# More filling products on TensorE between the end of the expert search and the first expert's rows

## The chip, the cores and the metric

The kernel runs on one core of one Trainium2 chip. The metric is the device time in microseconds (us) of one execution. One execution was also recorded by the hardware profiler; its rows are what this text reads. Five engines work side by side: PE (TensorE, matrix products; PEld is its weight load), DVE (VectorE), ACT (ScalarE), POOL (GpSimd, which here also issues the gathers) and SP (SyncE, which issues plain DMAs).

## The reference

A small language-model layer: embedding, attention, then a mixture of experts in which each expert chooses its tokens. What matters here is the last part (cut):

```python
N = B * S                                    # 8 * 512 = 4096 tokens, D = 256
k = max(MIN_CAPACITY, ceil(N * 2.0 / E))     # E = 8 experts, k = 1024
scores = softmax(xt @ Wr)
G, idx = top_k(scores.T, k)                  # each expert takes its 1024 best tokens
X_in = xt[idx]
h = gelu(einsum('ekd,edh->ekh', X_in, W1) + b1)       # 256 -> 1024
X_e = einsum('ekh,ehd->ekd', h, W2) + b2              # 1024 -> 256
out = zeros.at[idx].add(G * X_e)
```

## The kernel before, in words

`build_attention` does the attention and takes the first 60% of the time. `build_middle` does the router, the choice of tokens and the experts. Each engine has a hand-written list of instructions; they meet only through semaphores, and each engine works through its own list strictly in the order written. The part that the change touches runs from about 775 to 800 us of the span, in these steps:

1. **Search.** DVE and ACT count scores above a threshold; PE adds the counts over partitions (`total`, L1524) in 14 rounds. After each round PE does three filling products.
2. **Ranks.** PE multiplies once more (L1591, semaphore `ranked`), DVE computes ranks (`marked`), PE transposes them (L1597, semaphore `turned`).
3. **Lists.** For expert 0, DVE and ACT write two one-hot tensors (`hot_a`, `hot_b`), and PE turns them into a list of token numbers with 32 small products into `l_ps` (`write_list`, L1605, semaphore `listed`). DVE copies the list out (L1309 to L1316, semaphore `tok_ready`), and only then may it and PE do the same for expert 1.
4. **Rows.** As soon as a list is there, POOL issues eight indirect DMAs of 128 rows each (`gather`, L1036). The first four of expert 0 have a semaphore each (`first_in0` to `first_in3`), on which PE waits.
5. **First turn.** `first_turn` transposes each 128 rows on PE (L1625) into `x_ps` and `up`. ACT copies them out as the high part of a split float (L1415, `e_xT0hi`), DVE forms the low part (L1322, `e_xT0lo`).
6. **Experts.** For each of 16 steps of an expert PE does `up` (six products of 512 columns; `first_up`, L1636, for the first step, L1650 after it) and, two steps later, `down` (twelve products of 256 columns, L1662). Between them ACT applies Gelu twice (L1495 `hid`, L1498 `hT_hi`) and DVE forms `hT_lo` (L1322). Step 2's `up` waits for step 0's `hT_hi`, step 3's for step 1's.

The filling products are `warm(n)`: n products of the first expert's weights with themselves, 128x128 by 128x512, into the bank `y_ps[0][1]`. Nobody reads the result and nobody waits for it; the bank is written anew when the experts start. They show as `L1520 y<-w_0hi` in the trace. They wait for nothing, but PE's list is in order, so whatever stands behind them waits until they are through.

Of the kernel before, what the change touches and what calls it, by code (L numbers as in the profile page):

```python
# [802 lines left out]
def build_middle(nc, a, ident, h2, x2, wr_pair, early_lT, score, score_rows, shared):  # L803

    ctx = ExitStack()
    with ctx:
# [101 lines left out]
        def after(eng, name, count):  # L908

            if isinstance(count, int) and count <= 0:  # L910
                return
            eng.wait_ge(s[name], count)
# [593 lines left out]
        def _(pe):  # L1506
# [10 lines left out]
            def warm(n):  # L1517

                for _ in range(n):
                    nc.tensor.matmul(y_ps[0][1][:], w1[0][0][:, 0, 0:P], w1[0][0][:, 0, 0:HALF],  # L1520
                                     start=True, stop=True)

            def total(which, n):
                return nc.tensor.matmul(l_ps[:, 0:n], groups[:, which, :], count_bf[:, 0:n],  # L1524
                                        start=True, stop=True)
# [54 lines left out]
            for r in range(ITERATIONS):  # L1580
                pe.wait_ge(s["act_counted"], r + 1)
                for n in range(2):
                    nc.tensor.matmul(l_ps[:, 2:3], groups[:, 2, :], count_act[:, n:n + 1],
                                     start=n == 0, stop=n == 1)
                pe.wait_ge(s["counted"], r + 1)
                total(0, 2).then_inc(s["totalled"], 1)
                warm(3)
            pe.wait_ge(s["counted"], ITERATIONS + 1)
            for k, terms in enumerate([((0, 0), (1, 1)), ((1, 0), (1, 1))]):
                for n, (which, col) in enumerate(terms):  # L1590
                    last = nc.tensor.matmul(l_ps[:, 4 + k:5 + k], groups[:, which, :],  # L1591
                                            count_bf[:, col:col + 1], start=n == 0, stop=n == 1)
            last.then_inc(s["ranked"], 1)
            warm(12)
            pe.wait_ge(s["marked"], 1)
            for c in range(2):
                last = nc.tensor.transpose(x_ps[:, c * P:(c + 1) * P], rank[:, c, :], ident[:])  # L1597
            last.then_inc(s["turned"], 1)

            def write_list(e):  # L1600

                after(pe, "hot_ready", e + 1)
                after(pe, "tok_ready", e)
                for t in range(NB):
                    last = nc.tensor.matmul(l_ps[0:LIST_A, 0:2 * LIST_A], hot_a[:, t, :],  # L1605
                                            hot_b[:, t, 1:3, :].rearrange("p k b -> p (k b)"),
                                            start=t == 0, stop=t == NB - 1)
                last.then_inc(s["listed"], 1)
# [10 lines left out]
            def first_turn():  # L1619

                for c in range(TB):
                    warm(2)
                    pe.wait_ge(s[f"first_in{c}"], 16)
                    for kt in range(KT):
                        last = nc.tensor.transpose(first_x_ps[kt][:, c * P:(c + 1) * P],  # L1625
                                                   got[0][:, c, kt * P:(kt + 1) * P], ident[:])
                        if c == TB - 1:
                            last.then_inc(s["e_xt_tr"], 1)
                warm(2)
# [36 lines left out]
                            stop=dt == DT - 1 and c % 2 == 1 and n == 2)  # L1666
                last.then_inc(s["down_done"], 1)

            warm(16)
            pe.wait_ge(s["hot_b0"], 1)  # L1670
            write_list(0)
            warm(18)
            write_list(1)
            first_turn()

            def body(e, i, more, more2):
                for t in range(STEPS):
                    if t == 0:
                        after(pe, "w_lo2", 2 * e + 2)
                        if e > 0:  # L1680
                            after(pe, "e_xt_lo", 4 * e + 1)
                    if t == DT:
                        after(pe, "e_xt_lo", 4 * e + 4)
                    if e == 0 and t == 0:
                        first_up()
                    else:
                        up(e, i, t)
                    if e == E - 1 and t >= DT + LAG:
                        continue
                    if t >= LAG:  # L1690
                        down(e, i, t - LAG)
                    elif not (isinstance(e, int) and e == 0):
                        down(e - 1, 1 - i, STEPS + t - LAG)
                    if more2 and t == (4 if e == 0 else 2):
                        write_list(e + 2)
                    if more and 11 <= t < 15:
                        turn(e + 1, 1 - i, t - 11)
                    if e == 0 and t in (5, 6):
                        turn(0, 0, t - 3)
            experts(pe, body)  # L1700
            e = E - 1
            after(pe, "y_b2", e * 4)
            for c in range(TB):
                for dt in range(DT):
                    t = DT + dt
# [69 lines left out]
```

## Time and profile before

| | us |
|---|---|
| three timed runs | 1199.5, 1201.84, 1203.94 |
| median | 1201.84 |
| the profiled execution, its own time | 1200.93 |
| its span, first to last instruction | 1198.7 |

So 2.2 us of the profiled execution lie around its span. A timeline row gives the start in us from the start of the span, how long the row lasts, engine, line, operation, what is written and read, the shape, and the count of merged instructions; in brackets stands the idle time of the engine just before, and what ended it. PE rows overlap, since products are pipelined, and their ends are modelled. PEclk is the granted TensorE clock, 1.00 for 2.4 GHz and 0.50 for 1.2 GHz.

### The profile page before, as it was taken

What the parts mean: (1) busy time and instruction counts of PE and PEld (TensorE: products, weight loads), DVE (VectorE), ACT (ScalarE), POOL (GpSimd) and SP (SyncE); (2) the same over time, 40 slices, a digit from 0 to 9 for tenths busy, and PEclk for the clock granted to TensorE, in tenths of its full rate; (3) what the DMA queues carried; (4) which work ended last, traced back from release to release, by engine and by line L of the source; (5) the groups of instructions that cost most, each with busy time, mean ns of one, the idle gap of its engine ahead of it and who ended that gap; (6) DMA issues with size and microseconds to landing.
All of it is one profiled execution on the core that took longest, in us unless ns stands there. A gap on an engine that the chain in (4) does not pass through costs nothing. (4 is left out here: it accounts for less than half of the span.)

```text
span 1198.7 us, 20289 instructions
## 1 busy us (share of the span) xinstructions
PE 1142.1 (95%) x7083; PEld 999.6 (83%) x7083; DVE 818.8 (68%) x1972; ACT 720.7 (60%) x1533; POOL 825.4 (69%) x926
## 2 busy tenths in 40 slices
PE   3899999999999999999999998878999999999997
PEld 2788888888888888888888885558999999999996
DVE  4787887887887887887887766854555554554433
ACT  3667677677686686676676765315465555555642
POOL 3897898897897897897997864052484574654425
PEclk9999999999999999999999999789999999999999
DMA  5000100100100100100101003321362442523223
GB/s 197 1 18 2 45 28 1 45 27 1 45 27 2 45 28 1 54 18 9 63 1 36 19 1 112 110 66 39 94 138 32 115 124 32 130 39 104 32 23 36
DMA packets 42213, 58.12 MB, mean 48 GB/s; under 512 B 8896, under 2 KB 34944, under 8 KB 41984
## 3 DMA queue, kind: packets, MB, share of 16 engines
q0 software_dynamic: 13824, 21.24, 9.9%
q1 hardware_dynamic: 28288, 35.58, 8.8%
q8 instruction: 57, 0.93, 0.3%
q14 instruction: 44, 0.36, 0.1%
HBM read 35.71 MB, written 16.91 MB: 44 GB/s over the span
## 5 line engine op out<-in xcount | busy, mean ns | idle before, releaser
L278 ACT ACTIVATE prob<-prob,row_min 128x512 f32<-128x512 f32 (+3 forms) x256 | 141.8, 557 | 108.3 <-DVE row_min L468 108.3
L1322 DVE TENSOR_TENSOR hT_lo<-hid,hT_hi 128x512 fp32r<-128x512 f32 x124 | 86.2, 695 | 172.9 <-ACT hT_hi L1498 156.1
L1495 ACT ACTIVATE hid<-up,b_e 128x512 f32<-128x512 f32 x128 | 88.1, 688 | 158.9 <-PE up L1650 138.7
L214 POOL TENSOR_TENSOR q_sin<-q_sin,rope_t 128x512 f32<-128x512 f32 x64 | 82.8, 1293 | 84.0 <-ACT q_sin L302 84.0
L206 POOL TENSOR_SCALAR prob<-prob,row_inv 128x512 f32<-128x512 f32 (+3 forms) x256 | 134.5, 540 | 7.9 <-DVE row_inv L481 5.9
L1036 POOL DMA_INDIRECT x<-routed_rows,tokens x64 | 80.7, 1262 | 79.6 <-DVE tokens L1316 38.1
L403 DVE TENSOR_TENSOR pT_lo<-bank,pT_hi 128x384 fp32r<-128x384 f32 (+1 forms) x192 | 110.7, 596 | 18.4 <-ACT pT_hi L260 17.2
L1047 POOL TENSOR_SCALAR y<-y,gate 128x256 f32<-128x256 f32 x60 | 32.2, 548 | 127.1 <-issue 126.3
L1056 POOL DMA_INDIRECT out<-y,tokens x60 | 98.6, 1643 | 16.2 <-issue 13.9
L682 PE MATMUL bank<-ident,prob 128*128 128x128 f32 x640 | 101.9, 274 | 4.8 <-POOL prob L206 4.7
L260 ACT ACTIVATE pT_hi<-bank 128x384 fp32r<-128x384 f32 (+1 forms) x192 | 96.4, 518 | 13.6 <-PE bank L682 13.3
L468 DVE CUSTOM_DVE_ANT_0 prob<-bank,mask_row 128x512 f32<-128x512 f32 (+2 forms) x192 | 101.4, 554 | 2.0
L621 PE MATMUL bank<-kT_both,qT_hi 128*128 128x512 f32 (+2 forms) x384 | 99.7, 340 | 0.8 <-issue 0.5
L226 POOL TENSOR_TENSOR kT_both<-k_cos,kT_both 128x512 fp32r<-128x512 f32 x64 | 85.1, 1330 | 5.7 <-ACT kT_both L260 5.7
L220 POOL TENSOR_TENSOR q_cos<-q_cos,q_sin 128x512 f32<-128x512 f32 x64 | 82.7, 1293 | 5.0
L621 PEld LDWEIGHTS bank<-kT_both,qT_hi 128*128 128x128 f32 x384 | 71.4, 189 | 17.5 <-DVE row_min L468 1.1
L682 PEld LDWEIGHTS bank<-ident,prob 128*128 128x128 f32 x640 | 75.9, 140 | 11.0 <-POOL prob L206 8.8
L226 POOL TENSOR_TENSOR qT_lo<-q_cos,qT_hi 128x512 fp32r<-128x512 f32 x64 | 83.0, 1298 | 2.9 <-ACT qT_hi L260 2.9
L1498 ACT ACTIVATE hT_hi<-up,b_e 128x512 fp32r<-128x512 f32 x124 | 84.6, 682 | 0.0
L621 PE MATMUL bank<-wo_hi,oT_hi 128*128 128x256 f32 x256 | 81.9, 320 | 2.5 <-DVE oT_lo L403 2.5
L621 PE MATMUL bank<-pT_hi,v_hi 128*128 128x512 f32 (+3 forms) x256 | 82.8, 323 | 0.4 <-DVE pT_lo L403 0.4
L220 POOL TENSOR_TENSOR k_cos<-k_cos,k_sin 128x512 f32<-128x512 f32 x64 | 83.0, 1297 | 0.0
(318 smaller groups left out, 3887.9 us busy)
## 6 DMA issues: line engine op xcount, KB each, us to landing
raw<-in_w SPq DMA_DIRECT2D x16, 1024.0 KB
emb_res<-emb SPq DMA_DIRECT2D x8, 512.0 KB, 3.8
out<-h SPq DMA_DIRECT2D x8, 512.0 KB, 2.9
routed_rows<-x SPq DMA_DIRECT2D x8, 512.0 KB, 3.0
x<-in_wq SPq DMA_DIRECT2D x1, 1024.0 KB
x<-in_wk SPq DMA_DIRECT2D x1, 1024.0 KB, 5.1
x<-in_wv SPq DMA_DIRECT2D x1, 1024.0 KB, 7.3
x<-in_wo SPq DMA_DIRECT2D x1, 1024.0 KB, 10.2
```

The costliest lines, as they stand in the source:

```text
L206: nc.gpsimd.tensor_scalar(pr, pr, row_inv[:, h % 2, k:k + 1], 1.0, ALU.mult, ALU.mult).then_inc(s["norm_done"], 1)
L220: nc.gpsimd.tensor_tensor(cos[:], cos[:], sin[:], ALU.add).then_inc(s[f"{x}_add"], 1)
L226: nc.gpsimd.tensor_tensor(out[1][:, h % 2, :], cos[:], out[0][:, h % 2, :].bitcast(F32), ALU.subtract).then_inc(s[f"{x}_lo"], 1)
L260: nc.scalar.activation(out, in_, ACT.Copy).then_inc(s[name], 1)
L278: nc.scalar.activation(pr, pr, ACT.Exp, bias=row_min[:, h % 2, k:k + 1], scale=-1.0, accum_out=row_sum[:, h % 2, k:k + 1]).then_inc(s["exp ...
L403: nc.vector.tensor_tensor(out, in_, hi.bitcast(F32), ALU.subtract)\
L468: nc.vector.tensor_tensor_reduce(prob[:, h % 2, col:col + w], s_ps[bk][:, pc:pc + w], added, scale=-1.0 / D, scalar=3e38, op0=ALU.add, op1 ...
L621: last = nc.tensor.matmul(out, l, r, start=start and c == 0, stop=stop and c == len(todo) - 1)
L682: last = nc.tensor.transpose(t_ps[f][:, c * P:(c + 1) * P], prob[:, h % 2, col:col + P], ident[:])
L1056: pool.indirect_dma_start(a["out"][:, :], bass.IndirectOffsetOnAxis(tokens[e][:, TB * half + c:TB * half + c + 1], 0), y[half][:, c, :], N ...
L1322: nc.vector.tensor_tensor(out, in_, hi.bitcast(F32), ALU.subtract)\
L1495: nc.scalar.activation(hid[:, t % 2, :], up_ps[t % 2][:], ACT.Gelu, bias=bias)
```

## The change

Seven places get more filling products, 23 in all: 3 between the last search round and the last count, 3 before the transposes of the ranks, 4 before the first list, 5 before the second list, 4 between the products of the second list (one ahead of each eight), and 4 in `first_turn`, one before each of its four waits.

```diff
                 total(0, 2).then_inc(s["totalled"], 1)
                 warm(3)
+            warm(3)
             pe.wait_ge(s["counted"], ITERATIONS + 1)
...
             last.then_inc(s["ranked"], 1)
-            warm(12)
+            warm(15)
             pe.wait_ge(s["marked"], 1)
...
-            def write_list(e):
+            def write_list(e, filled=0):
 
                 after(pe, "hot_ready", e + 1)
                 after(pe, "tok_ready", e)
                 for t in range(NB):
+                    if filled and t % filled == 0:
+                        warm(1)
                     last = nc.tensor.matmul(l_ps[0:LIST_A, 0:2 * LIST_A], hot_a[:, t, :],
...
                 for c in range(TB):
-                    warm(2)
+                    warm(3)
                     pe.wait_ge(s[f"first_in{c}"], 16)
...
-            warm(16)
+            warm(20)
             pe.wait_ge(s["hot_b0"], 1)
             write_list(0)
-            warm(18)
-            write_list(1)
+            warm(23)
+            write_list(1, 8)
             first_turn()
```

The order of the other engines is the same. On PE, this is the stretch from the second list to the first expert's rows before (`y<-w_0hi` are the filling products, `l_ps<-hot_b,hot_a` the list, `x_ps` and `up` `<-ident,x` the transposes):

```order
L1520 MATMUL y<-w_0hi 128x512 x18
L1605 MATMUL l_ps<-hot_b,hot_a 32x64 x32
L1520 MATMUL y<-w_0hi 128x512 x2
L1625 MATMUL x_ps<-ident,x 128x128
L1625 MATMUL up<-ident,x 128x128
L1520 MATMUL y<-w_0hi 128x512 x2
```

And now; one of the 24 at the top stands behind the wait for the second list's one-hots, the other 23 ahead of it:

```order
L1520 MATMUL y<-w_0hi 128x512 x24
L1608 MATMUL l_ps<-hot_b,hot_a 32x64 x8
L1520 MATMUL y<-w_0hi 128x512
L1608 MATMUL l_ps<-hot_b,hot_a 32x64 x8
L1520 MATMUL y<-w_0hi 128x512
L1608 MATMUL l_ps<-hot_b,hot_a 32x64 x8
L1520 MATMUL y<-w_0hi 128x512
L1608 MATMUL l_ps<-hot_b,hot_a 32x64 x8
L1520 MATMUL y<-w_0hi 128x512 x3
L1628 MATMUL x_ps<-ident,x 128x128
L1628 MATMUL up<-ident,x 128x128
```

The list is cut into four, and each pair of transposes has three filling products ahead of it instead of two. From the last search round to the first list, on PE, before (`l_ps<-count_bf,groups` is the last count, `x_ps<-ident,x` the transposes of the ranks):

```order
L1524 MATMUL l_ps<-count_bf,groups 128x2
L1520 MATMUL y<-w_0hi 128x512 x3
L1591 MATMUL l_ps<-count_bf,groups 128x1 x4
L1520 MATMUL y<-w_0hi 128x512 x12
L1597 MATMUL x_ps<-ident,x 128x128 x2
L1520 MATMUL y<-w_0hi 128x512 x16
```

And now:

```order
L1524 MATMUL l_ps<-count_bf,groups 128x2
L1520 MATMUL y<-w_0hi 128x512 x6
L1592 MATMUL l_ps<-count_bf,groups 128x1 x4
L1520 MATMUL y<-w_0hi 128x512 x15
L1598 MATMUL x_ps<-ident,x 128x128 x2
L1520 MATMUL y<-w_0hi 128x512 x20
```

3, 12 and 16 became 6, 15 and 20, and the real products between them kept their order.

## Rows read from the trace of the kernel before

**Rows 1.** The page: busy time of each engine; the chain by engine.

```profile
PE 1142.1 (95%) x7083; PEld 999.6 (83%) x7083; DVE 818.8 (68%) x1972; ACT 720.7 (60%) x1533; POOL 825.4 (69%) x926
...
PE 33%; DVE 2%; issue 2%; ACT 1%; another core or an unknown queue 0%; POOLq 0%; DVEq 0%; ACTq 0%
```

**Rows 2.** Timeline of PE from the last search round to the first expert.

```profile
774.92 0.94 PE L1520 MATMUL y<-w_0hi 128*128 128x512 f32 x3
776.52 0.25 PE L1591 MATMUL l_ps<-count_bf,groups 128*128 128x1 bf16 x4 [0.66 <-DVE x L1246]
776.64 2.97 PE L1520 MATMUL y<-w_0hi 128*128 128x512 f32 x12
780.12 0.44 PE L1597 MATMUL x_ps<-ident,x 128*128 128x128 f32 x2 [0.51 <-DVE x L1267]
780.32 3.90 PE L1520 MATMUL y<-w_0hi 128*128 128x512 f32 x16
785.07 1.09 PE L1605 MATMUL l_ps<-hot_b,hot_a 128*32 128x64 bf16 x32 [0.85 <-DVE hot_b L1302]
786.09 4.38 PE L1520 MATMUL y<-w_0hi 128*128 128x512 f32 x18
791.48 1.11 PE L1605 MATMUL l_ps<-hot_b,hot_a 128*32 128x64 bf16 x32 [1.02 <-DVE hot_b L1302]
792.52 0.73 PE L1520 MATMUL y<-w_0hi 128*128 128x512 f32 x2
793.09 0.27 PE L1625 MATMUL x_ps<-ident,x 128*128 128x128 f32 x1
...
793.77 0.27 PE L1625 MATMUL x_ps<-ident,x 128*128 128x128 f32 x1
...
795.52 0.33 PE L1625 MATMUL x_ps<-ident,x 128*128 128x128 f32 x1 [0.20 <-issue]
...
799.92 0.77 PE L1636 MATMUL up<-e_xT0hi,w_0hi 128*128 128x512 f32 x1 [3.49 <-issue]
```

**Rows 3.** Timeline of DVE: both lists copied out of PE's bank.

```profile
786.20 0.18 DVE L1309 COPY list_tok<-l_ps 32x32 f32<-32x32 f32 x1
...
794.87 0.18 DVE L1309 COPY list_tok<-l_ps 32x32 f32<-32x32 f32 x1 [3.44 <-remote]
...
795.30 0.86 DVE L1316 CAST tokens<-list_f 32x8 int32<-32x8 f32 x4
```

**Rows 4.** Timeline of ACT: first expert's rows, then its first two Gelus.

```profile
799.17 0.60 ACT L1415 ACTIVATE e_xT0hi<-x_ps 128x512 fp32r<-128x512 f32 x1 [15.34 <-issue]
...
804.21 0.69 ACT L1495 ACTIVATE hid<-up,b_e 128x512 f32<-128x512 f32 x1 [3.73 <-issue]
...
810.48 0.69 ACT L1495 ACTIVATE hid<-up,b_e 128x512 f32<-128x512 f32 x1 [5.01 <-remote]
```

**Rows 5.** Timeline of PE: products of steps 1, 2 and 3 of the first expert.

```profile
804.32 0.63 PE L1650 MATMUL up<-e_xT0lo,w_0hi 128*128 128x512 f32 x1
...
804.75 0.45 PE L1650 MATMUL up<-e_xT0hi,w_0lo 128*128 128x512 f32 x1
...
806.10 0.39 PE L1650 MATMUL up<-e_xT0hi,w_0lo 128*128 128x512 f32 x1
...
811.80 0.80 PE L1650 MATMUL up<-e_xT0hi,w_0hi 128*128 128x512 f32 x1 [3.18 <-ACT hT_hi L1498]
```

**Rows 6.** Timeline of POOL: gathers of expert 0, expert 1's first and last.

```profile
788.26 1.35 POOL L1036 DMA_INDIRECT x<-routed_rows,tokens  x1 [36.93 <-DVE tokens L1316]
...
798.97 0.95 POOL L1036 DMA_INDIRECT x<-routed_rows,tokens  x1 [0.30 <-issue]
...
808.46 0.95 POOL L1036 DMA_INDIRECT x<-routed_rows,tokens  x1 [0.30 <-issue]
```

**Rows 7.** Stretches: length, busy us (instructions) of PE, PEld, DVE, ACT, POOL, PEclk.

```profile
794.80:798.20 3.40, 1.42 (x7) 0.55 (x5) 1.18 (x6) 0.00 (x0) 2.49 (x4) 0.97 0.36 96
798.20:801.60 3.40, 1.68 (x4) 1.38 (x5) 1.38 (x2) 1.20 (x2) 2.48 (x4) 0.50 0.40 113
```

## The prediction

> **What bounds the kernel now.** I read the page first. PE is busy 95% of the span, and of the chain that ended last the largest part, 33%, is PE [rows 1]. So for most of the time work added to PE would cost what it lasts. But the change touches only some 25 us between 775 and 800, and there the question is another: which wait ends last. So the second view is the timeline of PE in that stretch [rows 2]. PE never has enough real work there. It does filling products, then waits: 0.66, 0.51, 0.85 and 1.02 us for DVE, later 0.20 for the fourth gather, and 3.49 us before the first expert's first product. The third view is the timelines of DVE and ACT, because the reader should see something odd in them. The first list's last product ends, by the modelled end, at 785.07 + 1.09 = 786.16, and DVE copies the list at 786.20. The second ends at 791.48 + 1.11 = 792.59, and DVE copies it only at 794.87, 2.3 us late [rows 2, 3]. The fourth transpose ends at 795.85, and ACT copies at 799.17, 3.3 us late. Step 1's products end at 805.20, and ACT begins its Gelu at 810.48, 5.3 us late [rows 2, 4, 5]. In each case the late engine waits only for PE. All of it falls into the time in which POOL issues its 16 gathers, 788.26 to 809.41 [rows 6]. I don't know the mechanism; I call it **the late signals**. PE's step 3 starts at 811.80, released by ACT's second `hT_hi`, and so 5.3 us of late signal stand right ahead of it [rows 4, 5].
>
> **The price of one filling product.** 16 of them last 3.90 us, and one alone shows 0.39, so they start (3.90 - 0.39) / 15 = 0.234 us apart at the full clock [rows 2]; the 0.39 is that of a product of the same shape at the full clock, the last row but one of its group [rows 5]. The half clock makes it 0.43, from the spacing 804.75 - 804.32 of products of that shape [rows 5]. The clock is full through all of the stretch to 798.2 (0.97 to that point, 0.50 behind it) [rows 7]. What stands behind n filling products can start n x 0.234 after their first.
>
> **Part by part, the first four.**
> - 3 before the last count. Six now start at 774.92: the next product is free at 774.92 + 1.40 = 776.32, and it started at 776.52, since it waits for DVE. Cost nothing.
> - 15 instead of 12 before the transposes: 776.64 + 15 x 0.234 = 780.15, against 780.12 now. Cost 0 to 0.03, on the path, since DVE waits for these transposes.
> - 20 instead of 16 before the first list: 780.32 + 4.68 = 785.00, against 785.07. Nothing.
> - 23 instead of 18 before the second list: 786.09 + 5.38 = 791.47, against 791.48. Nothing.
> These four groups are as long as the waits that they fill. The cover is DVE's work on ranks and one-hots, and a different product spacing by 1% would move each by 0.05, so I take 0.1 for all four, with 0 and 0.3 as ends (0.3 if each of the three long groups ends 0.1 late) [rows 2].
>
> **The second list.** Its waits come first, then a filling product ahead of each eight. Each costs its 0.234 and a change of operands: behind the list the next filling product starts at 792.52, where the list's own 32 starts end at about 792.43, so 0.09 more [rows 2]. Four make 0.94 to 1.30; I take 1.3. The list ends at 793.9 instead of 792.6. Its signal is for DVE (`tokens` of expert 1). POOL needs them at 798.97 and has them, by the last cast, at 796.16: 2.8 us to spare, which 1.3 fits into [rows 3, 6]. DVE's next work behind it waits for ACT's copy, which begins at 799.17 [rows 4]. Were the signal late by more, the next bound would be POOL's second gather.
>
> **The first turn.** Before, the first transpose was at 793.09, 0.57 behind the start of its two filling products; now it is 1.3 + 0.234 later, 794.6. To the fourth there are three more groups, each of which took 793.77 - 793.09 = 0.68 and now takes 0.68 + 0.234 = 0.91: 794.6 + 2.74 = 797.35. The fourth was at 795.52, held by its gather [rows 2]. So the fourth transpose comes **1.8 us later** on PE. That is the one delay of the change which is not filled waiting time. What stands behind it: ACT's copy, DVE's low part, the first product, and step 0 and 1 of the expert.
>
> **Is the 1.8 us on the path?** By the timeline it ends at 797.35 + 0.33 = 797.7, and ACT started at 799.17 [rows 4]. If the signal comes when something outside PE lets it (POOL's gathers), there are 1.5 us of cover; what remains, 0.3, must get past step 1, whose result waited 5.3 us for its signal, to the 810.48 that stood at POOL's end (809.41). Then nothing is left. If each signal is late by a fixed time behind PE's end, the whole 1.8 comes through. Bounds 0 and 1.8; I take 0, because the lateness is not fixed in the rows: 2.3, 3.3, 1.4 (step 0's sixth product starts 5 x 0.43 behind 799.92 and shows 0.63, so it ends near 802.8; ACT begins at 804.21) and 5.3 [rows 2 to 5]. A fixed delay would show one number.
>
> A rule speaks against this choice. The Trainium skill, page "Perfetto Trace Analysis", section "Tensor Engine Instruction (MATMUL, LD_WEIGHTS)", says that a product's end is computed, not observed, and that the semaphore follows only when PSUM has acknowledged the bytes. By that page the late signals can be an array behind its records, and then every filling product delays them. By it the sum would be the 1.8 us of the first rival; the unequal lateness above does not decide it.
>
> **The clock.** Now PE works until about 798.1 without a gap, where before it was busy 1.42 of 3.40 us in 794.8 to 798.2, and the grant fell to half at 798.2 [rows 7]. So it may fall later. Twelve products of the expert's first two steps ran at 0.43 apart instead of 0.234 [rows 5]: 12 x 0.196 = 2.3 us is the most it gives. But these two steps end in the same late signal at 810.48, so I book 0 for it.
>
> **Sum.** 0.1 + 0 + 0 = +0.1 us. The profiled execution took 1200.93 (span 1198.7), 0.9 under the median 1201.84 of the three runs; set on the median it gives 1201.9, rounded to **1202.0**.
>
> **The rivals.**
> - *Slower: the filling products are in the signals' way.* The mechanism is the one fixed delay behind the fourth transpose; it decides if ACT's copy comes at 799.17 + 1.8 = 801.0 and step 1's Gelu behind 812. Price +1.8, time 1203.7. For it: it is the one place where real work is pushed back past its own data. Against: the unequal lateness. 24%.
> - *Faster: the clock stays up.* If step 1's Gelu follows PE and not POOL, the first two steps gain up to 2.3 us, less the 0.3 left of the later start: -2.0, time 1199.8. For it: the drop at 798.2 stands behind the one gap that the change fills. Against: PE is still idle from about 798 to 800, and the grant may just fall a little later. 14%. The Trainium skill, page "TensorE: Matmul & The Clock Gate", section "Why this matters for your kernels", advises against idle gaps between bursts of products, because the clock falls back; it would make this rival the likely one.
> - *Much faster: the late signals go.* They start just at the second list, into which filling goes. Without them: fourth transpose done at 797.7, two copies of 0.6 and DVE's low parts to 799.6, step 0's products to 800.1, Gelu pair 1.3, steps 1 and 2 and the twelve of `down` behind it (1.4 + 1.4) to 804.3, against 811.80 [rows 2, 4, 5]: -7.5, time 1194.3. For it: three runs of the same kernel lie 4.4 us apart, so something in it varies. Against: nothing in the change touches the gathers. 9%, half of it for a part of this gain only.
> - *The change doesn't do what it says:* the grant falls as before, and nothing moves at all. Same time, 3%.
>
> **How the numbers follow.** Forecast 50%, slower rival 24%, clock 14%, signals 9%, no effect 3%. Two in ten are to be left out: half of the signals' rival lies below 1196.0, and above 1205.0 lie the slower rival's upper part (1203.7 with 1.3 for a median of few runs). Between them lie all ends of the terms, with the runs' own spread. Range 1196.0 to 1205.0. A measurement of this kernel can tell about 0.5% from no change, 6 us. Only the full gain of the signals' rival goes beyond: faster 0.08, slower 0.04 (a late list that reaches POOL's second gather, or a mechanism not seen here), same 0.88.
>
> **What would show it.** In the changed kernel's timeline: the waits of 0.66, 0.51, 0.85 and 1.02 are nearly gone and the products behind them start at the same times; the second list lasts about 2.3 us; the fourth transpose stands near 797.4. If the hiding is right, ACT's first copy is at 799.2 to 799.6, its second Gelu within 0.5 of 810.5 and POOL's gathers where they were. A copy near 801 and a Gelu behind 812 are the slower rival. A PEclk of 1.00 through 801 with the Gelu before 809 is the clock's. A Gelu near 802 is that of the signals. The prediction is wrong if the ends of the four first groups lie over 0.3 us behind, or if a difference stands outside 775 to 815.

## Result and profile after

| | before | after |
|---|---|---|
| median of 20 timed runs each | 1201.29 us (1197.02 to 1203.94) | 1205.14 us (1202.34 to 1206.73) |
| profiled execution, its own time | 1200.93 | 1206.37 |
| its span | 1198.7 | 1204.2 |

The change makes the kernel slower: ratio 1.0035, 95% interval [1.0026, 1.0044], so 3.1 to 5.3 us. That is within the 0.5% that I had called no change, but outside the stated range, just above its end, and it is a clear loss where I had forecast +0.1 us.

The spans differ by 5.5 us. The first 0.9 us are there before the changed code: the filling products behind the last search round start at 775.81 and stood at 774.92, and the first list starts at 785.96 and stood at 785.07 [rows 2], so nothing is added between the two. So I read the rows of after with 0.9 taken off. The other 4.6 us arise between 786 and 835 us; from the first expert's step 8 to the end both kernels take 368.6 us.

The timeline of PE after, which answers to [rows 2, 5] (start, duration, engine, line, operation, tiles, shape, count, idle time before it and its releaser):

```profile
775.81 1.63 PE L1520 MATMUL y<-w_0hi 128*128 128x512 f32 x6
...
781.21 4.79 PE L1520 MATMUL y<-w_0hi 128*128 128x512 f32 x20
785.96 1.09 PE L1608 MATMUL l_ps<-hot_b,hot_a 128*32 128x64 bf16 x32
786.98 5.90 PE L1520 MATMUL y<-w_0hi 128*128 128x512 f32 x24
792.81 0.41 PE L1608 MATMUL l_ps<-hot_b,hot_a 128*32 128x64 bf16 x8
793.14 0.50 PE L1520 MATMUL y<-w_0hi 128*128 128x512 f32 x1
793.58 0.41 PE L1608 MATMUL l_ps<-hot_b,hot_a 128*32 128x64 bf16 x8
...
795.12 0.41 PE L1608 MATMUL l_ps<-hot_b,hot_a 128*32 128x64 bf16 x8
...
796.25 0.27 PE L1628 MATMUL x_ps<-ident,x 128*128 128x128 f32 x1
...
797.17 0.27 PE L1628 MATMUL x_ps<-ident,x 128*128 128x128 f32 x1
...
799.00 0.27 PE L1628 MATMUL x_ps<-ident,x 128*128 128x128 f32 x1
...
805.12 0.77 PE L1639 MATMUL up<-e_xT0hi,w_0hi 128*128 128x512 f32 x1 [5.27 <-issue]
...
809.34 0.40 PE L1653 MATMUL up<-e_xT0hi,w_0lo 128*128 128x512 f32 x1
813.51 0.80 PE L1653 MATMUL up<-e_xT0hi,w_0hi 128*128 128x512 f32 x1 [3.77 <-ACT hT_hi L1498]
```

The four waits for DVE are gone or too short to be shown, as intended. But the wait before the expert's first product grew from 3.49 to 5.27 us. Who is late is seen on DVE and ACT, which answer to [rows 3, 4]; the second list's copy, the copies of the expert's rows, and the first three Gelus:

```profile
796.54 0.18 DVE L1309 COPY list_tok<-l_ps 32x32 f32<-32x32 f32 x1 [4.22 <-PE l_ps L1608]
```

```profile
804.38 0.60 ACT L1415 ACTIVATE e_xT0hi<-x_ps 128x512 fp32r<-128x512 f32 x1 [19.65 <-remote]
804.87 0.59 ACT L1415 ACTIVATE e_xT0hi<-up 128x512 fp32r<-128x512 f32 x1
812.19 0.69 ACT L1495 ACTIVATE hid<-up,b_e 128x512 f32<-128x512 f32 x1 [6.72 <-remote]
812.78 0.68 ACT L1498 ACTIVATE hT_hi<-up,b_e 128x512 fp32r<-128x512 f32 x1
813.35 0.69 ACT L1495 ACTIVATE hid<-up,b_e 128x512 f32<-128x512 f32 x1
```

The last transpose ends at 799.27; ACT copies 5.1 us behind it, where it was 3.3 us before. Step 0's products end near 808.0; its Gelu starts 4.2 us behind them. In before, step 0's signal got through (804.21) and step 1's was held until 810.48; now step 0's is held too: its Gelu starts at 812.19, 2.7 us behind the end of POOL's last issue, and step 1's signal is there by then. A stretch in which such a signal stays out I call **the hold**. POOL's last gather, and the stretches of after in the columns of [rows 7]:

```profile
808.56 0.95 POOL L1036 DMA_INDIRECT x<-routed_rows,tokens  x1 [0.30 <-issue]
```

```profile
798.20:801.60 3.40, 1.65 (x10) 1.03 (x8) 0.00 (x0) 0.00 (x0) 2.49 (x4) 1.00 0.34 94
801.60:805.00 3.40, 0.00 (x0) 0.00 (x0) 0.00 (x0) 0.62 (x2) 2.49 (x4) 0.53 0.38 111
805.00:808.40 3.40, 3.28 (x8) 2.63 (x9) 1.29 (x2) 0.47 (x1) 2.65 (x3) 0.50 0.44 119
```

The columns are the stretch, its length, the busy us (instructions) of PE, PEld, DVE, ACT and POOL, PEclk, the DMA share and GB/s. The clock did stay at full level for longer, through 801.6, but PE had nothing to do then, and its first real products at 805.12 ran at half level all the same.

### The profile page after: what moved, and what is told of

Same layout as the page of the kernel before. It is cut to its first block and busy times, and to the rows that moved or that the text cites. A ratio compares the mean times of both kernels' runs of the same rounds, so it can differ in the third digit from the quotient of the medians.

```text
span 1204.2 us, 20335 instructions
## 1 busy us (share of the span) xinstructions
PE 1146.6 (95%) x7106; PEld 1003.8 (83%) x7106; DVE 817.8 (68%) x1972; ACT 720.0 (60%) x1533; POOL 822.8 (68%) x926
## 5 line engine op out<-in xcount | busy, mean ns | idle before, releaser
L682 PEld LDWEIGHTS bank<-ident,prob 128*128 128x128 f32 x640 | 76.0, 140 | 10.8 <-POOL prob L206 8.4
```

Of the source, the lines that this page charges most:

```text
L682: last = nc.tensor.transpose(t_ps[f][:, c * P:(c + 1) * P], prob[:, h % 2, col:col + P], ident[:])
```

## The experiments

Sixteen kernels, in four sets, each set on one chip beside runs of the kernel before. "Late" is always the start of the instruction that waits, less the modelled end of PE's product that it waits for. The ratios are measured as such and are not quite those of the two medians; a time in us beside a ratio is that share of before's median in the same set. Two terms: the *turn's* filling products are those in and behind `first_turn`; the *list's* are those between the products of the second list.

### First set: the parts of the change alone, and no filling at all

**e1_four**, the four groups ahead of the lists only:

```diff
             warm(3)
+            warm(3)
...
-            warm(12)
+            warm(15)
...
-            warm(16)
+            warm(20)
...
-            warm(18)
+            warm(23)
```

> The change's first four groups alone (6, 15, 20 and 23 products), the second list and the first turn as before. Theory A (the cost sits where real products are pushed back: the second list and the first turn): within 0.5 us of before, ACT's first copy of the expert's rows and its second Gelu as late behind PE as before (3.3 and 5.3 us). Theory B (these groups run over their waits and hold up the ranks or the first list): 0.5 to 2 us slower, with the first gather later behind the end of the search. Theory C (any filling product more while POOL issues gathers makes PE's signals later): 1 to 2 us slower, ACT's first copy more than 4 us behind the last transpose.

Measured: ratio 1.0003 [0.9986, 1.0019]. List copied 2.3 us late, rows 2.7 us. The interval, -1.7 to +2.3 us, doesn't shut out theory B by itself; the trace does. From the last count of the search to the first list pass 10.2 us, here (775.59 to 785.76) as before (774.89 to 785.07). Theory C's copy over 4 us late isn't there. So theory A holds for these groups: filling these waits on DVE costs nothing, and that goes for the five products more ahead of the second list too, which run to 792.30, when POOL has issued gathers since 788.97.

**e2_list**, the list's four only:

```diff
-            write_list(1)
+            write_list(1, 8)
```

> Before, with only the four filling products between the products of the second list. Theory A: the list ends 1.3 us later, and the last transpose about 0.95 us later (a waiting time of 0.35 is used up); ACT's copy moves by that much if the signals are late by a fixed time: +1.0 us in all. Theory C: +1 to +2 us. If the late signals end when POOL lets them: 0.

Measured: ratio 1.0025 [1.0012, 1.0038], 3.0 us slower (1.4 to 4.6), more than theory A's 1.0; the interval still touches C's 1 to 2. The rows are 3.9 us late, and step 0's Gelu waits until 809.97, 1.9 us behind POOL's last issue, which ends at 808.08. So this group alone already puts step 0 into the hold.

**e3_turn**, the first turn's four only:

```diff
-                    warm(2)
+                    warm(3)
                     pe.wait_ge(s[f"first_in{c}"], 16)
```

> Before, with only the four filling products more in the first turn (three ahead of each wait instead of two). Last transpose 0.94 - 0.35 = 0.6 us later. Theory A with a fixed lateness: +0.6 us. Theory C: +1.5 to +3 us, with ACT's copy over 4 us behind the last transpose. If the late signals end when POOL lets them: 0.

Measured: ratio 1.0001 [0.9988, 1.0015]; rows 3.5 us late. No loss is seen; theory C's least, 1.5 us, is just within the interval, and a fixed lateness (+0.6) can't be told from none.

**e4_nofill**, no filling products from the second list on:

```diff
-            warm(18)
             write_list(1)
...
-                    warm(2)
                     pe.wait_ge(s[f"first_in{c}"], 16)
...
-                warm(2)
```

> Before, without any filling product from the second list on (the 18 ahead of it, the 2 ahead of each wait of the first turn and the 2 behind it are gone; no result changes). If filling products make PE's signals late: DVE copies the second list at once (under 0.2 us behind its last product), ACT copies the rows at once, and the kernel is 3 to 7 us faster, in spite of a half clock in the first steps. If the gathers alone make them late: the signals are as late as before (2 to 5 us), and the time is within 1 us of before, or up to 2 us slower by the half clock.

Measured: ratio 0.9943 [0.9924, 0.9962], median 1192.56: 4.6 to 9.1 us faster. The rows' copy is 0.5 us late instead of 3.3, and the first expert's first product starts 12.0 us behind the first list's (784.36 to 796.38) instead of 14.9 (785.07 to 799.92). The second list's signal was still 1.5 us late, with no filling product near it, so the gathers do a part by themselves. The clock was at half level for 6.8 us from 786.9 and for 3.4 us from 797.1, and the kernel was faster all the same. The filling products are the cause of most of the lateness, and the kernel before already paid for its own.

### Second set: which filling products, and what of them

**e5_turn_free** keeps the 18 ahead of the second list, and drops the turn's ten:

```diff
-                    warm(2)
                     pe.wait_ge(s[f"first_in{c}"], 16)
...
-                warm(2)
```

> Before, keeping the 18 filling products ahead of the second list, without any in or behind the first turn. Theory F (filling products done while gathers are in flight hold PE's signals back, the ones nearest the signal most): ACT copies the rows under 1 us behind the last transpose, and most of the 8.4 us is won, -6 to -8. Theory G (what counts is the 18 ahead of the list, since they start the hold): the list's signal is 2.3 us late and the rows' too, within 1.5 us of before.

Measured: ratio 0.9929 [0.9915, 0.9943], 6.8 to 10.2 us faster. Rows 1.1 us late, where theory F had under 1. Theory F holds, G doesn't.

**e6_list_free** drops the 18 and keeps the turn's ten:

```diff
-            warm(18)
             write_list(1)
```

> Before, without the 18 filling products ahead of the second list, those of the first turn (10) kept. Theory F: ACT's copy stays about 3 us late, and the time is within 2 us of before. Theory G: ACT's copy is under 1 us late and the time 6 to 8 us lower.

Measured: ratio 0.9994 [0.9981, 1.0006]; rows 2.0 us late, where theory F had about 3. In time it is theory F again: with the ten kept, the 18 neither help nor hurt, and without the ten (e5) nearly everything is won.

**e7_gather_late** keeps every filling product but holds back expert 1's gathers:

```diff
             gather(0, 0)
+            pool.wait_ge(s["h_hi"], 3)
             gather(1, 1)
```

> Before with all its filling products, but POOL issues expert 1's eight gathers only after the expert's third Gelu pair (expert 0's eight as before, to about 797.7). If gathers in flight are needed for late signals: the list's and the rows' signals stay late (2 to 3 us), but step 0's and step 1's Gelu follow PE's products at once (under 0.3 us), and the kernel is 4 to 7 us faster. If filling products alone do it: no change.

Measured: ratio 0.9988 [0.9977, 1.0], so at most 2.8 us faster, not the 4 to 7. But the timeline of ACT says more than the time. The Gelus of steps 0, 1 and 5:

```profile
803.03 0.69 ACT L1496 ACTIVATE hid<-up,b_e 128x512 f32<-128x512 f32 x1 [2.65 <-PE up L1637]
803.61 0.68 ACT L1499 ACTIVATE hT_hi<-up,b_e 128x512 fp32r<-128x512 f32 x1
805.12 0.69 ACT L1496 ACTIVATE hid<-up,b_e 128x512 f32<-128x512 f32 x1 [0.83 <-PE up L1651]
...
820.06 0.69 ACT L1496 ACTIVATE hid<-up,b_e 128x512 f32<-128x512 f32 x1 [6.07 <-remote]
```

and POOL's last of expert 0 and its held gathers, first and last:

```profile
797.10 0.95 POOL L1036 DMA_INDIRECT x<-routed_rows,tokens  x1 [0.30 <-issue]
808.61 1.16 POOL L1036 DMA_INDIRECT x<-routed_rows,tokens  x1 [10.55 <-ACT hT_hi L1499]
...
817.76 0.95 POOL L1036 DMA_INDIRECT x<-routed_rows,tokens  x1 [0.30 <-issue]
```

With no gather in flight, step 0's and step 1's Gelus follow PE within 0.1 us. The hold is gone there. It came back where the gathers now are: step 5's products end at 816.7, and its Gelu starts at 820.06, 1.4 us behind the end of POOL's last issue at 818.71. No filling product is near that place. So it takes gathers in flight for the hold, and it needs no filling products; the time was moved, not won. The rows' copy, still among expert 0's gathers, was 4.0 us late here.

**e8_narrow**: the filling products from the second list on have 64 columns instead of 512, in the same number:

```diff
+            def warm(n, cols=HALF):
...
+                    nc.tensor.matmul(y_ps[0][1][:, 0:cols], w1[0][0][:, 0, 0:P], w1[0][0][:, 0, 0:cols],
...
-                    warm(2)
+                    warm(2, 64)
...
-            warm(18)
+            warm(18, 64)
```

> Before, with the same number of filling products from the second list on, but of 64 columns instead of 512. If the number of PE instructions holds the signals back: as late as before, time within 1 us. If the columns (what they read and write) do it: like the kernel without filling products, signals under 1.6 us late, -6 to -9 us.

Measured: ratio 1.0012 [0.9997, 1.0028]; rows 3.4 us late, though the products move an eighth of the columns. So the columns don't hold the signals; as many products hold them as long, whatever their width.

### Third set: where in the turn, and the best version

**e9_best**: the change's four groups, no filling in the list or the turn (edits to the changed kernel).

```diff
-                    warm(3)
...
-                warm(2)
...
-            write_list(1, 8)
+            write_list(1)
```

> The change's first four groups (6, 15, 20 and 23), the second list's products without filling, and none in or behind the first turn. If only the filling products of the first turn matter: as in e5_turn_free, -7 to -9 us against before. If the first four groups cost something once nothing hides them: -5 to -7.

Measured: ratio 0.9954 [0.9938, 0.9970], median 1194.11; rows 0.5 us late. That is 3.6 to 7.4 us faster, 6.3 by the medians, which is the second of the two expectations. Its interval and e5's still overlap, so a cost of the first four groups isn't shown by it.

**e10_no_tail**, without the two behind the last transposes:

```diff
-                warm(2)
```

> Before without the two filling products behind the last transposes; the eight ahead of the waits stay. Theory H (the products right behind a signalling one hold its signal): ACT's copy under 1.2 us late, -5 to -8 us. Theory I (the queue of filling products and gather waits ahead of it does it): as before, within 1 us.

Measured: ratio 0.9980 [0.9967, 0.9993], 0.8 to 4.0 us faster: short of theory H's 5 to 8, and only the end of the interval touches theory I's 1. Rows 2.7 us late, as theory I has it. So the two behind the transposes take a small part of the time.

**e11_no_between**, without the eight ahead of the four waits:

```diff
-                    warm(2)
                     pe.wait_ge(s[f"first_in{c}"], 16)
```

> Before without the eight filling products ahead of the four waits; the two behind the last transposes stay. Theory H: ACT's copy about 3 us late, within 1.5 us of before. Theory I: under 1.2 us late, -6 to -8 us.

Measured: ratio 0.9957 [0.9943, 0.9972]; 3.4 to 6.8 us faster; rows 0.04 us late. These eight cost most; theory I holds, H doesn't. The timeline of PE at the third and fourth transpose, and of ACT:

```profile
793.83 0.33 PE L1624 MATMUL x_ps<-ident,x 128*128 128x128 f32 x1 [0.75 <-DMA x<-routed_rows,tokens]
...
795.18 0.33 PE L1624 MATMUL x_ps<-ident,x 128*128 128x128 f32 x1 [0.92 <-DMA x<-routed_rows,tokens]
```

```profile
795.55 0.60 ACT L1415 ACTIVATE e_xT0hi<-x_ps 128x512 fp32r<-128x512 f32 x1 [12.10 <-PE x_ps L1624]
```

PE waits for each gather, and the copy starts with the end of the last transpose, 795.51.

**e12_after_turn_free**: the changed kernel, the list's four included, without the turn's (edits to the changed kernel).

```diff
-                    warm(3)
...
-                warm(2)
```

> The changed kernel with all its groups, the four between the products of the second list too, but none in or behind the first turn. Theory A (position only: the list's four push the transposes back by 1.3 us): 1 to 1.5 us slower than e9_best, since here signals come at once. If a filling product between list products holds the signals by itself: 3 us or more slower than e9_best, with ACT's copy over 2 us late.

Measured: ratio 0.9979 [0.9967, 0.9991]; rows 2.6 us late; median 3.4 us above e9's. The last transpose hardly moved against e9's: it ends 10.9 us behind the first list's start (786.31 to 797.17), and 10.8 us in e9 (786.19 to 796.98). So this isn't theory A's 1 to 1.5 us of transposes pushed back: the list's four hold the signals by themselves.

### Fourth set: the whole put together

**e13_after_gather_late**: the changed kernel with e7's edit.

```diff
+            pool.wait_ge(s["h_hi"], 3)
             gather(1, 1)
```

> The changed kernel, with expert 1's eight gathers issued only after the third Gelu pair, as in e7_gather_late. If the change loses because step 0's signal is held until expert 1's gathers have landed: step 0's and step 1's Gelu within 0.3 us of PE's products, and only 0 to 1.8 us slower than e7_gather_late (1200 to 1201). If the gathers are not the cause: over 4 us slower than e7_gather_late.

Measured: ratio 0.9981 [0.9970, 0.9993], median 1199.14, against e7's 0.9988 [0.9977, 1.0]. So the change's loss isn't seen any more once expert 1's gathers aren't in flight. The Gelus of steps 0 and 1:

```profile
801.59 0.69 ACT L1496 ACTIVATE hid<-up,b_e 128x512 f32<-128x512 f32 x1 [1.48 <-PE up L1640]
...
802.92 0.69 ACT L1496 ACTIVATE hid<-up,b_e 128x512 f32<-128x512 f32 x1
```

They follow PE within 0.1 us. Both kernels wait again at step 5, for the moved gathers, so their equal times alone would say little; but already step 0's Gelu is no later than in e7, 17.6 us behind the first list's start (783.99 to 801.59) against 18.6 (784.47 to 803.03). The rows' copy, at 799.02, is 1.7 us late, where it was 5.1 in the changed kernel; POOL's last issue of expert 0 had ended at 797.56. And here the longer filling did keep the clock: the first products soon start 0.23 us apart, at full level, where in e7 they started 0.43 us apart from 800.59 on.

```profile
799.77 0.47 PE L1640 MATMUL up<-e_xT0hi,w_0hi 128*128 128x512 f32 x1 [1.87 <-ACT e_xT0hi L1416]
...
800.31 0.39 PE L1640 MATMUL up<-e_xT0hi,w_0hi 128*128 128x512 f32 x1
800.54 0.39 PE L1640 MATMUL up<-e_xT0hi,w_0lo 128*128 128x512 f32 x1
```

**e14_ahead**: the kernel before with the turn's eight all ahead of its first wait.

```diff
+                warm(8)
                 for c in range(TB):
-                    warm(2)
                     pe.wait_ge(s[f"first_in{c}"], 16)
```

> Before with the eight filling products of the first turn all ahead of its first wait, none between the waits; same number, same two behind. If standing between the waits is what matters: like e11_no_between, 6 to 7 us faster, copy under 0.5 us late. If the number of products ahead of the signal within the gathers matters: as before, within 1.5 us, copy 2 to 4 us late.

Measured: ratio 0.9990 [0.9981, 1.0]; rows 2.8 us late. Where the eight stand, ahead of the waits or between them, makes no difference that is seen.

**e15_after_no_list**: the changed kernel without the list's four.

```diff
-            write_list(1, 8)
+            write_list(1)
```

> The changed kernel without the four filling products between the products of the second list. If the list's four are the loss: within 1 us of before, step 0's Gelu before 808. If the first turn's four are: 3 to 4 us slower than before.

Measured: ratio 1.0019 [1.0010, 1.0028], between the two expectations: 2.3 us slower (1.2 to 3.4); rows 3.7 us late, step 0's Gelu at 810.28. So the list's four aren't the whole loss. The first four groups (e1) and the turn's four (e3) show no cost each, though their intervals reach up to 2.3 and 1.8 us; if they cost more together than apart, and why, is open. ACT shows one thing that the table below leaves out: the second copy of the rows comes 2.1 us behind the first, 5.7 us behind its transpose, which ends at 797.41.

```profile
801.01 0.60 ACT L1415 ACTIVATE e_xT0hi<-x_ps 128x512 fp32r<-128x512 f32 x1 [16.26 <-remote]
803.14 0.60 ACT L1415 ACTIVATE e_xT0hi<-up 128x512 fp32r<-128x512 f32 x1 [1.53 <-remote]
```

**e16_last_two**: the kernel before with the list's and the turn's four.

```diff
-                    warm(2)
+                    warm(3)
...
-            write_list(1)
+            write_list(1, 8)
```

> Before with the list's four and the first turn's four, not the first four groups. If these two groups make the whole loss: 4 us slower than before, as the changed kernel, with step 0's Gelu only behind the last gather's landing. If the first four groups take part: 2 to 3 us slower.

Measured: ratio 1.0025 [1.0016, 1.0034]; rows 5.9 us late, step 0's Gelu at 812.33, as in the changed kernel. By the medians it is the whole loss, by the ratio two thirds, and its interval reaches the changed kernel's ratio.

### What the runs say together

The lateness of the rows' first copy against the number of filling products between the second list's start and the last transposes (one profiled execution each):

| filling products | kernels | rows' copy late, us |
|---|---|---|
| 0 | e4, e5, e9, e11 | 0.5, 1.1, 0.5, 0.0 |
| 4 | e12 | 2.6 |
| 8 | before, e1, e6, e10, e14, e8 (narrow), e7 | 3.3, 2.7, 2.0, 2.7, 2.8, 3.4, 4.0 |
| 12 | e3, e15, e2 | 3.5, 3.7, 3.9 |
| 16 | e16, after | 5.9, 5.1 |
| 16, gathers over by 797.56 | e13 | 1.7 |

On the whole a filling product adds about 0.3 us of lateness to the rows' signal, beside its own 0.23 us or so, though kernels with the same number lie up to 2 us apart. Shown: it takes gathers in flight (e7, e13), and it goes neither by the size of the products (e8) nor by their place in the turn (e14). Without gathers in flight, filling products hold nothing: the first list's copy at 786.20 comes 0.04 us behind 16 of them and the list [rows 2, 3].

Four things in the same traces warn against taking 0.3 us as the price of a product.

- **The signals come in steps.** From the second list's copy to the rows' first copy pass 1.43 us in e9, 2.15 in e5, 2.86 in e12, 3.6 in e1 and e10, 4.3 in before, 5.0 in e3, e6, e7 and e8, 5.72 in e2, 7.84 in after and 8.6 in e16. These are about 2, 3, 4, 5, 6, 7, 8, 11 and 12 times 0.715. The three not named (e13, e14, e15) lie up to 0.12 us off such a step, and only e11, where PE waited longest for its data, lies well off. So more filling seems to move a signal by whole steps of some 0.7 us; what sets them isn't known.
- **The second list's signal does not follow the rule.** Its copy comes 3.4 us behind the list's first product, both where the list lasts 1.1 us (before) and where it lasts 1.9 (e4, e6, e8, at half clock). With the four filling products in the list (after, e2, e12, e16, e13) it is only 1.0 to 1.1 us behind the last product instead of 2.3.
- **Without filling the gathers still hold signals, only later.** In e5, step 3's Gelu starts at 812.34, 4.8 us behind PE's products, in the last stretch of expert 1's gathers.
- **PE's idle time changed too.** Ahead of the last transposes PE waited 0.77 to 0.92 us for the gather in e5, e9 and e11, 0.30 us in e4, and at most 0.23 us in the others. No run tells the number of filling products from a pause that lets the signals catch up.

A single execution also says little on its own: e1 has before's filling products from the second list on, and its profiled execution took 4.1 us less than before's from the last count of the search to the end (774.89 to 1198.7 before, 775.59 to 1195.3 in e1), while the medians of e1 and before differ by 1.5 us and the ratio is 1.0003. The verdicts rest on the ratios.

Not shown is what in the chip does it. Two readings were there. One is an array that is behind its records. Against it: in after, step 0's Gelu waits until 812.19, and step 1's starts at 813.35 without any wait, 1.16 us later, while the six products between the two signals take 6 x 0.234 = 1.4 us even at the full clock; the trace's semaphore records, which the views don't print, put the two signals 0.07 us apart (812.11 and 812.18). And the granted clock of after fell to half near 801.8, behind a stretch in which the records show PE idle, and while the rows' signal was still out. Both fit products that were done and signals that were held; neither is a test. The Trainium skill, page "Perfetto Trace Analysis", section "Tensor Engine Instruction (MATMUL, LD_WEIGHTS)", has the semaphore updated only upon PSUM's acknowledgement, behind the computed end; the traces agree that the signal may come behind it, by up to 6.7 us here (step 1 in e6, 802.78 to 809.50), and no run tells if it is that acknowledgement which is held.

## The prediction, step by step

- **The first four groups cost 0 to 0.3: right.** e1 gives 1.0003, the four waits are used up and no more, and the first list still starts 10.2 us behind the last count.
- **The price of a filling product, 0.234: right** within a run of them (796.25 to 797.17 is 0.92 per group, as forecast). **Between list products it was mis-sized.** The list's blocks follow each other by 793.58 - 792.81 = 0.77, where eight list products alone take 0.24. So one costs 0.53, not 0.325, and the list ended 2.0 us later, not 1.3.
- **The fourth transpose 1.8 us later: mis-sized** by the same 0.7. It stands at 799.00, less 0.9 is 798.1, against 797.35 foreseen: 2.6 us later.
- **"Is the 1.8 us on the path?": this step failed.** I took 0 with 1.8 as the upper bound. I saw four unequal latenesses (2.3, 3.3, 1.4, 5.3) and concluded that PE's own timing didn't set them. What I left out is that the lateness could depend on what PE is given to do. It goes up with the filling products: 3.3 became 5.1. So ACT's copy moved by 804.38 - 0.9 - 799.17 = 4.3 us, more than my upper bound. Unequal latenesses spoke against one fixed delay, but not for a fixed end, and I had no third case between 0 and 1.8. The rows of before could not show it, since the filling stands ahead of every late signal in them; it takes a kernel with other filling (e5, e11, e16).
- **The cover behind it was also misread.** I counted 5.3 us of wait at step 1 as slack, since the gathers' end at 809.41 stood fixed. Held signals do come near that end, but not at it: 1.1 us behind the end of POOL's last issue in before, 1.9 in e2, 1.4 in e7 and 2.7 in after (809.51 to 812.19). And before, step 0 had come out of the hold at 804.21, so that step 2's products and step 0's `down` ran within it, in 805.5 to 808.6. With the start later by 4.3 us, step 0 is in the hold as well, and step 2 starts at 813.51 instead of 805.52. Less the 0.9 that is 7.1 us later: behind the hold there is one more step to do. After some of it is regained, 4.6 us are left.
- **The second list's tokens had room: right.** The gathers of expert 1 were not held up: the last is issued at 808.56, and 808.46 before.
- **The slower rival had the right place and side, but the wrong mechanism and price:** +1.8 from a fixed delay, against about +4. Its marks were a copy near 801 and step 1's Gelu behind 812; less the 0.9, that Gelu came at 812.5, as it said, and the copy at 803.5.
- **The clock rival fell.** The grant fell later, as it assumed, but PE had no work in the stretch that this won, because its first product waited for ACT's late copy. In e13, where that copy came sooner, the products did run at full level.
- **The rival that the late signals go** had the right price (-7.5) for another change. e4, e5, e9 and e11 reach it by taking filling away: medians 1192.56 to 1194.11, ratios 0.9929 to 0.9957.

The fastest of the kernels run are e4, e5, e9 and e11, all without the eight filling products ahead of the gather waits and without any in the second list. Their intervals lie from 0.9915 to 0.9972 of before and overlap or touch, so which of them is best isn't shown.

## What to carry to other kernels

A filling product isn't free because the engine would wait anyway: count also what it does to the signals of the real products behind it. In this kernel, where indirect gathers are in flight and another engine waits for PE, it paid to leave PE idle; filling the waits on DVE cost nothing. And where a trace shows signals that come long behind the work they tell of, do not book the gap as slack before a run has shown what sets it.

## What was not expected of the hardware

- PE's signals came up to 6.7 us behind its products while POOL's gathers were in flight, and within 0.1 us where none were (e7, e13). Those of steps 0 and 1 that were held for 5 us or more (before, e2, e3, e6, e14) came 0.9 to 2.8 us behind the end of POOL's last issue; those of the rows came while POOL was still issuing, in steps of some 0.7 us.
- Eight products that nobody reads, in front of the gather waits, cost 5 us (e11, 3.4 to 6.8); with an eighth of the columns, filling from the second list on cost no less (e8).
- A filling product between products of 64 columns costs 0.53 us, twice what it takes in a row of its like.
- More filling did not mean less half clock: from 786 to 805 us the granted clock was at half level for 6.8 us in before, and for 3.4 us in e5, e9 and e11, which have less filling. Only e4, without any, has it for 10.2 us, and it is as fast as they are.
